# One group in the MLP's TensorE loop, values' halves before the exponentials and x1n, Q's and C's weights a slot end later

## The reference

```python
# block 0, per item; c = 128 channels, t = s = 512 positions
Mn = Wn @ inorm(x) + bn;  Mm = Wm @ inorm(ctx) + bm
A  = softmax(Mn^T Mm, over s)                        # 512 x 512
x1 = Wo @ ((Wl @ ctx + bl) A^T) + bo + x
# block 1, per item; 128 rows of D = 512, 16 heads of 32
q = (layer_norm(x1) * ln1_w + ln1_b) @ q_w + q_b;  k = ctx @ k_w + k_b;  v = ctx @ v_w + v_b
hidden = softmax(mask(q k^T / sqrt(32))) v @ cproj_w + cproj_b + x1
out = hidden + gelu((layer_norm(hidden) * ln2_w + ln2_b) @ fc_w + fc_b) @ proj_w + proj_b   # 512 -> 2048 -> 512
```

## Time and profile before

| what | value |
|---|---|
| three runs, median (lowest, highest) | 3207.83 us (3205.83, 3208.77) |
| the profiled execution, its own time | 3204.95 us |
| its span, first to last instruction | 3202.9 us |
| mean granted TensorE clock | 0.986 of full |
| PE, share of the span busy | 96%, 19575 matmuls |
| DVE, ACT, POOL | 57%, 47%, 25% |
| instruction packets of q8 and q14 | 204 (3.34 MB), 21 (0.17 MB) |
| MLP's first transposes on PE | 1759 us |

### The profile page before, as it was taken

The page is one execution under the profiler, slowest core; times in us unless marked ns, Lnnn a source line. Parts: engine busy times, 40 slices in busy tenths (PEclk is TensorE's granted clock), DMA queues, the critical chain, the costliest instruction groups (busy, mean ns, idle before and its releaser), DMA issues. The chain is left out here.

```text
span 3202.9 us, 56096 instructions
## 1 busy us (share of the span) xinstructions
PE 3073.2 (96%) x19575; PEld 2595.2 (81%) x19575; DVE 1817.7 (57%) x3577; ACT 1498.1 (47%) x4210; POOL 798.1 (25%) x742
## 2 busy tenths in 40 slices
PE   6999999999999999999997999999999999999999
PEld 5888888888888888888885788787878878787887
DVE  5777777777777777777773533333333333333332
ACT  5777777777777777777774311111111111111111
POOL 3433333433443344444432100000000000000000
PEclk8999999999999999999998999999999999999999
DMA  4111111111111111111112311111110101111110
GB/s 125 45 53 51 51 51 50 51 51 51 52 52 51 51 50 51 51 51 50 50 34 62 102 33 38 40 40 40 40 36 18 40 28 39 40 40 41 40 27 14
DMA packets 232097, 150.43 MB, mean 47 GB/s; under 512 B 142912, under 2 KB 176192, under 8 KB 231872
## 3 DMA queue, kind: packets, MB, share of 16 engines
q1 hardware_dynamic: 231872, 146.91, 15.6%
HBM read 97.57 MB, written 33.55 MB: 41 GB/s over the span
## 5 line engine op out<-in xcount | busy, mean ns | idle before, releaser
L1212 ACT ACTIVATE gl<-pre,fc_bias 128x512 f32<-128x512 f32 x256 | 176.8, 691 | 1154.9 <-PE pre L1297 1154.9
L1251 DVE CAST hT_hi<-gl 128x512 fp32r<-128x512 f32 x256 | 109.2, 427 | 874.6 <-ACT gl L1212 874.6
L639 ACT ACTIVATE rows<-bank,negmax 128x128 f32<-128x128 f32 x1024 | 361.9, 410 | 110.5 <-DVE negmax L739 110.5
L1295 PE MATMUL pre<-yT_lo,rest_hi 128*128 128x512 f32 x768 | 298.8, 389 | 0.0
L1296 PE MATMUL pre<-yT_hi,rest_lo 128*128 128x512 f32 x768 | 298.8, 389 | 0.0
L1297 PE MATMUL pre<-yT_hi,rest_hi 128*128 128x512 f32 x768 | 298.8, 389 | 0.0
L1295 PE MATMUL acc<-rest_lo,hT_hi 128*128 128x512 f32 x768 | 298.8, 389 | 0.0
L1296 PE MATMUL acc<-rest_hi,hT_lo 128*128 128x512 f32 x768 | 298.8, 389 | 0.0
L1297 PE MATMUL acc<-rest_hi,hT_hi 128*128 128x512 f32 x768 | 298.7, 389 | 0.0
L562 POOL TENSOR_TENSOR rows<-rows,rsum 128x512 f32<-128x512 f32 x256 | 264.1, 1042 | 129.8 <-DVE rsum L735 125.9
L604 ACT ACTIVATE rows<-bank,negmax 128x512 f32<-128x512 f32 x256 | 175.1, 689 | 213.3 <-DVE negmax L756 213.3
(11 more groups left out here) (160 smaller groups left out, 7970.9 us busy)
## 6 DMA issues: line engine op xcount, KB each, us to landing
x_ctx_in<-in_x SPq DMA_DIRECT2D x64, 256.0 KB, 2.8
x_ctx_in<-in_ctx SPq DMA_DIRECT2D x64, 256.0 KB, 3.0
blocks<-in_ctx SPq DMA_DIRECT2D x256, 64.0 KB, 1.9
small<-in_x SPq DMA_DIRECT2D x64, 256.0 KB, 3.6
hidden<-hid SPq DMA_DIRECT2D x64, 256.0 KB, 2.0
rows<-hidden SPq DMA_DIRECT2D x16, 1024.0 KB, 5.5
out<-rows SPq DMA_DIRECT2D x64, 256.0 KB, 2.1
stage<-y SPq DMA_DIRECT2D x240, 64.0 KB, 2.1
```

The costliest lines, as they stand in the source:

```text
L639: act.activation(probs[:, r, c, :], by_chunk(S1_BANK[r])[:, c, :], ACT.Exp, bias=negmax1[:, r, c:c + 1], accum_out=sum1[:, r, c:c + 1]).th ...
L1212: act.activation(gl[:, i % 2, :], pre[i % 2][:], ACT.Gelu_apprx_tanh, bias=mlp.fc_bias[:, i:i + 1]).then_inc(gelu_done, 1)
L1295: pe.matmul(out, a_hi, b_lo, start=first, stop=False)
```

## The change

PE's loop in the MLP runs over one group, 14 times, between groups 0 and 15; a class `Single` with a period of 1 gives its semaphore values. The other engines keep their loop of two. ACT makes `outT_hi` before exp1(0) in place of after it; DVE makes `outT_lo` before x1n in place of after the fourth maximum and the first reciprocal. Q's halves are made at the end of slot 2 (ACT and DVE), C's upper halves at the end of ACT's slot 3, and C's lower halves in POOL's slot 3.

```diff
+class Single(Item):
+
+    period = 1
@@ POOL, slot
-                if b2.first():
+                if b3.first():
                     lower_halves(C_W)
                 if b3.exists():
                     for r in range(4):
@@ ACT, slot
-                if b2.first():
-                    upper_halves(Q_W)
-                    upper_halves(C_W)
...
-                exp1(0)
                 if b4.exists():
                     act.wait_ge(outT_done, b4.nth(1, 1))
                     act.activation(flat(outT_hi), bank[PV_BANK][:], ACT.Copy).then_inc(outT_hi_set, 1)
+                exp1(0)
                 exp1(1)
                 exp1(2)
                 exp1(3)
                 if b1.exists():
                     act.wait_ge(xnT_turned, b1.nth(1, 1))
                     act.activation(pair_half(xnT_hi, b1), by_chunk(XN_BANK), ACT.Copy).then_inc(xnT_hi_set, 1)
+                if b2.first():
+                    upper_halves(Q_W)
+                if b3.first():
+                    upper_halves(C_W)
@@ DVE, slot
                     dve.reciprocal(rsum0[:], sum0[:]).then_inc(rsum0_set, 1)
-                if b2.first():
-                    lower_halves_of_q()
...
                 maxima1(0)
                 maxima1(1)
+                if b4.exists():
+                    dve.wait_ge(outT_hi_set, b4.nth(1, 1))
+                    lower(flat(outT_lo), bank[PV_BANK][:], flat(outT_hi), outT_lo_set)
                 if b1.exists():
                     dve.wait_ge(x1_rstd_ready, b1.nth(1, 1))
...
                 sum1_reciprocal(0)
-                if b4.exists():
-                    dve.wait_ge(outT_hi_set, b4.nth(1, 1))
-                    lower(flat(outT_lo), bank[PV_BANK][:], flat(outT_hi), outT_lo_set)
                 sum1_reciprocal(1)
...
                     lower(pair_half(xnT_lo, b1), by_chunk(XN_BANK), pair_half(xnT_hi, b1), xnT_lo_set)
+                if b2.first():
+                    lower_halves_of_q()
@@ PE, MLP
-            def group(g, first):
+            def group(g):
...
-            groups(pe, group)
+            group(Item(0, 0, G))
+            with pe.Fori(0, G - 2) as turn_:
+                group(Single(turn_, 1, G))
+            group(Item(0, G - 1, G))
```

## The result

The changed kernel takes **3113.09 us** (median of 4 runs, 3111.93 to 3114.79) against 3206.83 (3203.82 to 3208.77) for the kernel before, measured beside it: a ratio of 0.9709, 95% interval 0.9692 to 0.9726. That is 93.7 us less. The forecast was 3115. The profiled execution took 3114.79 us, the slowest of the four; its span is 3112.8, so 90.1 less than the span before.

The account below looks back on a forecast made before the run. PE was taken to bound the kernel, through its waits on outT_lo and at MLP branches. From 3204.95 us, -35.5 (MLP), -52.4 (slots), -1.3 (tail), -3.7 (weights) gave 3112.05, plus 2.88 to the median: 3115 us, range 3100 to 3193.

Parts of the forecast that it names:

- What bounds the kernel: Whole kernel: only shortening PE's waits on outT_lo (39.1 us) and MLP "issue" (21.0 us), or start and tail losses, moves the end.
- MLP loop, -35.5: PE's MLP loop over one group: six taken branches of 5.92 us each stop costing, 35.5 us off.
- Kept: PE's one-group MLP body stays in its instruction buffer, so a taken branch costs 0.05 us, hidden by PE's queue.
- rival 2: MLP: PE's one-group body is not kept, so 13 branches cost 5.92 us each; 3192 us, chance 0.18.
- Values' halves, 0.80 a regular slot: Attention slots: earlier outT_hi and outT_lo save 0.80 us in each of 46 slots; all 59 slots give -52.4.
- x1n "would end at 1018.9 as now": Attention slot: x1n, started at 1018.48, still precedes POOL's change of instruction by 0.1 us and ends at 1018.9.
- Rival 1: Attention slots: x1n misses POOL's change of instruction, so a slot gains 0.28 us, not 0.80; 3146 us, chance 0.18.
- x1n with the same median: Attention slots: sign of success, x1n's median time unchanged at 1.06 us; 1.5 or above would show the late case.
- Branch intervals, 1.20: The 13 slots ending at a taken attention-loop branch gain 1.20 us each: 0.80 plus 0.4 from reaching it earlier.
- Weights, -3.7: Slots 2 to 4: later Q and C weights give -6.6 in slot 2, +0.85 and +2.05 later; -3.7 in all.
- The tail, -1.3: Three tail slots: the outT_lo wait shrinks, but exponentials bound them anyway; 1.3 us off (0 to 3).
- The sum: Whole kernel: 3204.95 - 35.5 - 52.4 - 1.3 - 3.7 = 3112.05 us profiled; with 2.88 for the median, 3115.

Follow-up runs that it names:

- e6: The changed kernel with already-fulfilled waits padding PE's MLP loop body to 1497 instructions in place of 793; 3318.38 us (one run).
- e7: The changed kernel with already-fulfilled waits padding PE's MLP loop body to 1561 instructions in place of 793; 3505.18 us (one run).
- e4: The changed kernel with DVE making x1n ahead of outT_lo in all slots; 3112.69 us, ratio 0.9706 to the kernel before.
- e2: The kernel before with only outT_hi moved ahead of exp1(0) on ACT and outT_lo ahead of x1n on DVE; 3154.88 us, ratio 0.9835.
- e2b: The kernel before with only DVE's outT_lo moved ahead of x1n, ACT's order unchanged; 3213.61 us (one run).
- e9: The changed kernel with three small one-column tensor_scalar instructions on DVE ahead of x1n in every slot; 3147.73 us (one run).
- e5: The changed kernel with a one-column memset on DVE between outT_lo and x1n in every slot; 3116.24 us (one run).

## Why the prediction was right

The mechanisms it named for the two large gains are the ones the runs show. That the time came within 2 us of 3115 is in part luck: x1n and the weights brought 8.4 and 1.2 us less than forecast, the branch intervals and the tail 5.6 and 0.9 more, and the medians lie 93.7 us apart where the two traces lie 90.1 apart.

- **What bounds the kernel**: right. Removing the two PE waits moved the end by nearly all that they and their surroundings were priced at.
- **MLP loop, -35.5**: -35.4 in the trace and -36.0 alone. "Kept" was right with room to spare: the body could nearly double. The branch takes 0.21 us, not 0.05, and is over the 0.15 that the prediction named as its sign; PE's queue hides it. Where the limit lies was open in it, between 3.1 and 6.1 blocks of 250; e6 and e7 put it between 6.0 and 6.2.
- **The loop is not kept (rival 2)**: did not hold; bodies of 793 and 1497 instructions branch in 0.21 us. By the rule of the Trainium skill ("Runtime: NRT & Kernel Launch", Instruction fetch mechanics), a branch out of a window of two blocks fetches, and these two would have; the trace does not agree with it.
- **Values' halves, 0.80 a regular slot**: 0.82.
- **x1n "would end at 1018.9 as now"**: this step failed where it was read. That end left x1n 0.42 us, less than the 0.54 that the prediction itself gives it alone; in the slots where it is in time it ends 2.15 us behind PV, in place of 2.09. And the slot of the earlier trace rows is a first one of the body, and there x1n starts at 1.66 us behind PV, exactly the predicted 1018.48 against 1016.82, with POOL's change of instruction 0.10 later; 0.10 was not enough, 0.13 in the other slots is. That slot does not stand for all: in the others the maxima end 0.05 us earlier, which the prediction did not know, so that x1n was in time in three slots of four is luck. Rival 1 held in the fourth, with a gain of 0.20 for its 0.28. On the 14 of them it took 14 x 0.60 = 8.4 us. The sign "x1n with the same median" did not come either: the median fell from 1.06 to 0.54, as x1n now starts 0.2 us before POOL's first instruction ends and not 0.8.
- **Branch intervals, 1.20**: 1.63. The prediction let the sequencer's lead grow by 0.4 of 0.5, taking the MLP's 3.35 us as its end. It grew by 0.8, from 2.9 to 3.7 us (branch at 4.16 us behind PV before with the queue dry at 7.0; at 2.49 and 6.2 after), because nothing holds the sequencer at `outT_lo` any more. e4 shows the link from the other side. That is 13 x 0.43 = 5.6 more. By these two errors the forecast's -52.4 - 1.3 = -53.7 becomes -50.9; e2 measured -51.0, closer than its own interval can tell. From PV of slot 5 to PV of slot 61 it was 50.0 forecast (43 x 0.80 + 13 x 1.20) and 47.75 measured.
- **Weights, -3.7**: -2.45. Slot 2 is the term that was mis-sized, -5.67 for -6.6: `u_lo` came 4.82 earlier (forecast 4.7) and the slow clock gave 2.2 (forecast 1.9), but in slot 2 x1n, which the larger wait had covered, is late by 1.5 next. Q's wait was 1.22 for 0.85, C's 1.84 for 2.05.
- **The tail, -1.3**: from PV of slot 61 to the MLP's first transposes the changed kernel takes 3.8 us less; two more slots at 0.80 and the tail's 1.3 made 2.9.
- **The sum**: spans 90.1 us apart, 92.9 forecast from the profiled execution. 54.8 of it lies ahead of the MLP (57.4 forecast) and 35.4 in it.

## What to carry to other kernels

A slot picked as a model should be checked against its neighbours in the loop: here the first slot of the loop's body differed by 0.05 us, and that decided 0.6. When the value PE waits for is moved, look at what it holds in the sequencer too: a wait that PE itself never feels can cost half a microsecond at each long branch. Where a value passes through two engines, look at both: here moving one side alone gave nothing.

## What the hardware showed that was not expected

- x1n (a DVE `tensor_scalar`, 128x512 float32) takes 0.54 us alone (e2b). Beside POOL's `normed_lo` it does not slow down in proportion: where it has to wait, it ends 0.28 us after the POOL instruction that runs, or the one behind it (before: at 2.09 us behind PV, with POOL's first ending at 1.81; e9: at 3.34 and 3.06). Started 0.13 us or more ahead of POOL's next instruction it gets in between, with 0.10 it waits that one out (1.68 us). `outT_lo` on the same DVE takes 0.68 beside a POOL instruction and 0.65 behind them.
- A PE loop of 1497 instructions branches in 0.21 us without fetching (e6); one of 1561 fetches about 8 packets of 16 KB a pass, and its branch takes 4.7 us (e7).
- A memset of one column between two DVE instructions moved the second one's start by 0.01 us (e5); three `tensor_scalar` of one column moved it by 0.18 (e9).
